# First attention of a gated two-layer block: scores and both mixes adjacent, one turn less depth, normalising on GpSimd, small inputs as rows

## The reference

```python
x = x + tanh(g_xattn[0]) * L0_xattn(ctx, layernorm(x), mask, ...)   # this step
x = x + tanh(g_ffn[0])   * L0_ffn(layernorm(x), ...)                # 16 experts
x = x + tanh(g_xattn[1]) * L1_xattn(layernorm(x), ctx, ctx, ...)
x = x + tanh(g_ffn[1])   * L1_ffn(layernorm(x), ...)

# L0_xattn: 8 heads of 64
c, l = layer_norm(ctx) * w + b, layer_norm(x') * w + b
q = l @ Wq;  k, v = split(concat([c, l]) @ Wkv)          # 128 keys per sequence
q, k = l2norm(q) * q_scale, l2norm(k) * k_scale           # per head
sim = 8 * q @ k.T, masked;  out = softmax(sim) @ v
y = layer_norm(out @ Wo) * w
```

## Time and profile before

| | |
|---|---|
| median of 3 runs | 402.84 us (402.82 to 404.82) |
| profiled execution, its time | 402.89 us |
| its span, first to last instruction | 401.1 us |
| mean granted clock of TensorE | 0.977 |
| PE, PEld busy | 370.6 (92%), 270.5 (67%) |
| DVE busy | 324.2 (81%) |
| ACT busy | 258.2 (64%) |
| POOL busy | 222.0 (55%) |
| DMA packets | 61035, 13.27 MB |

### The profile page before, as it was taken

The page is one execution under the profiler, slowest core; times in us unless marked ns, Lnnn a source line. Parts: engine busy times, 40 slices in busy tenths (PEclk is TensorE's granted clock), DMA queues, the critical chain, the costliest instruction groups (busy, mean ns, idle before and its releaser), DMA issues. The chain is left out here.

```text
span 401.1 us, 10527 instructions
## 1 busy us (share of the span) xinstructions
PE 370.6 (92%) x3589; PEld 270.5 (67%) x3589; DVE 324.2 (81%) x921; ACT 258.2 (64%) x514; POOL 222.0 (55%) x389
## 2 busy tenths in 40 slices
PE   7699989999999999999999999999799999997765
PEld 6356656666666676777756888778577777775554
DVE  2999999899889999987483788565658988887896
ACT  2477767787777777776654222344377777787784
POOL 3655668656676666663422000046738888886860
PEclk9999999999999999999999999999989999998599
DMA  5979999900000000000000000000000000000003
GB/s 162 260 145 123 124 129 126 95 2 2 0 2 2 2 2 2 1 2 2 3 2 0 2 0 0 2 2 0 2 2 2 2 2 2 3 2 2 1 15 92
DMA packets 61035, 13.27 MB, mean 33 GB/s; under 512 B 51108, under 2 KB 60344, under 8 KB 60984
## 3 DMA queue, kind: packets, MB, share of 16 engines
q1 hardware_dynamic: 60196, 12.37, 21.7%
q10 hardware_dynamic: 660, 0.23, 0.2%
q0 software_dynamic: 128, 0.00, 0.0%
HBM read 11.55 MB, written 1.05 MB: 31 GB/s over the span
## 5 line engine op out<-in xcount | busy, mean ns | idle before, releaser
L407 POOL TENSOR_TENSOR a_rn<-a_ssq,neghalf 128x8 f32<-128x8 f32 x48 | 79.0, 1654 | 23.2 <-DVE a_ssq L1019 18.6
L90 POOL TENSOR_TENSOR nrow<-mrow 128x2 f32<-128x2 f32 x32 | 6.3, 198 | 55.8 <-DVE mrow L86 55.5
L1019 DVE TENSOR_REDUCE a_ssq<-q_home 128x8 f32<-128x512 f32 x48 | 32.2, 672 | 5.4 <-ACT q_home L798 5.2
L501 PE MATMUL a_x<-wkv_a,a_kvT 128*128 128x512 f32 x64 | 34.5, 621 | 1.4 <-ACT a_kvT L791 1.0
L804 ACT ACTIVATE kv_home<-a_x,maskcol 128x512 f32<-128x512 f32 x32 | 21.9, 684 | 18.8 <-PE a_x L501 18.8
L1372 POOL TENSOR_TENSOR b_k<-b_ksb,quad 128x256 f32<-128x256 f32 x32 | 19.0, 614 | 12.0 <-ACT b_ksb L1723 12.0
L423 POOL TENSOR_TENSOR a_yr<-a_ymv,eps_row 128x1 f32<-128x1 f32 x16 | 3.1, 192 | 37.7 <-DVE a_ymv L1062 37.7
L1887 DVE TENSOR_REDUCE b_mx<-b_s 128x16 f32<-128x1024 f32 x16 | 19.6, 1224 | 5.1 <-PE b_s L1530 5.1
L1038 DVE TENSOR_REDUCE a_mx<-a_s 128x4 f32<-128x512 f32 x32 | 21.9, 685 | 2.0 <-PE a_s L527 1.9
L816 ACT ACTIVATE kv_home<-a_m,cols 128x512 f32<-128x512 f32 x32 | 21.9, 686 | 0.6 <-PE a_m L515 0.5
L546 PE MATMUL a_m<-kv_home,p_home 128*64 128x65 f32 x512 | 21.9, 228 | 0.3 <-ACT p_home L826 0.3
(11 more groups left out here) (298 smaller groups left out, 1149.6 us busy)
## 6 DMA issues: line engine op xcount, KB each, us to landing
w_gu<-in_L_ffn_Wg_dram SPq DMA_DIRECT2D x4, 512.0 KB, 9.4
w_gu<-in_L_ffn_Wu_dram SPq DMA_DIRECT2D x4, 512.0 KB, 11.5
w_d<-in_L_ffn_Wd_dram SPq DMA_DIRECT2D x8, 256.0 KB, 7.7
out_dram<-xs SPq DMA_DIRECT2D x8, 128.0 KB, 1.8
xs<-in_x_dram SPq DMA_DIRECT2D x1, 640.0 KB, 8.8
cs<-in_ctx_dram SPq DMA_DIRECT2D x1, 640.0 KB, 10.2
wkv_a<-in_L_xattn_Wkv_dram SPq DMA_DIRECT2D x2, 256.0 KB, 6.6
nat<-in_L_ffn_w_dram SPq DMA_DIRECT2D x2, 256.0 KB, 3.1
```

The costliest lines, as they stand in the source:

```text
L407: nc.gpsimd.tensor_tensor(rn[:, tp, i, :], ssq[:, tp, i, :], neghalf[:, 0:H0], ALU.pow)\
L501: nc.tensor.matmul(p_x[:], kvT[:, tp, b * 2 * S:(b + 1) * 2 * S], wkv_a[:, INNER:2 * INNER], start=True, stop=True).then_inc(vproj_done, 1)
L1019: nc.vector.tensor_reduce(ssq[:, tp, i, :], sq[:, i, :].rearrange("p (h d) -> p h d", h=H0), AX.X, ALU.add).then_inc(reduced, 1)
```

## The change

- TensorE: in a turn, both `mix` of tile s - 2 stand directly behind `scores` of tile s - 1 at the end of the turn, where the mixes of s - 3 stood apart at the start of the next. Both `probs_T` of s - 2 and `xT` of s + 1 come ahead of the scores.
- GpSimd normalises the tiles from 2 on; the mean is stored negated and added. Its powers are spread over the turn.
- VectorE's and ScalarE's lists are reordered; the squares' sums and the query scale of tile s move into turn s; `write_output`, `next_input` come one and two turns earlier, and there are 19 turns instead of 21. The statistics of the last group and the other extra work stay at the end of their turns.
- The prologue ends with operations of tiles 1 and 2 that were in the first turn.
- The mask comes once as rows and is cast into two halves of `small_rows`; the head scales are loaded as rows 32 and 33 of it, and one transpose turns them all, which now waits for the scales as well. On ScalarE's queue the masks go ahead of the second group of context.

```diff
-        maskraw = sb("maskraw", [B, 2 * S], U8)
-        mask_rows = sb("mask_rows", [B, 2 * S])
+        maskraw = sb("maskraw", [B, S], U8)
+        small_rows = sb("small_rows", [B + 2, 2 * S])
...
-        TURNS = range(2, NT + 7)
+        TURNS = range(2, NT + 5)
...
-            for i, w in ((8, q_scale), (9, k_scale)):
+            for i, w in enumerate((q_scale, k_scale)):
                 for a in range(2):
-                    pool.dma_start(cols[a * DH0:(a + 1) * DH0, i:i + 1],
-                                   w.rearrange("(d o) -> d o", o=1)).then_inc(scale_in, 16)
+                    pool.dma_start(small_rows[B + i:B + i + 1, a * DH0:(a + 1) * DH0],
+                                   w.rearrange("(o d) -> o d", o=1)).then_inc(scale_in, 16)
...
+            def normalise(t, tp):
+                wait(pool, xT_done, t - 1 if t > 2 else t)
+                nc.gpsimd.tensor_scalar(xn[:, tp, 0, :], cs[:, t, :], moments[:, 0, t, 0:1], moments[:, 0, t, 1:2],
+                                        ALU.add, ALU.mult)
+                nc.gpsimd.tensor_scalar(xn[:, tp, 1, :], xs[:, t, :], moments[:, 1, t, 0:1], moments[:, 1, t, 1:2],
+                                        ALU.add, ALU.mult).then_inc(xn_ready, 1)
+
             inverse_roots(0)
             inverse_roots(1)
             for i in range(3):
                 inverse_norm(0, 0, i)
-            inverse_roots(2)
+            pool.wait_ge(norms_ready, 2)
+            normalise(2, 0)
+            inverse_norm(1, 1, 0)
+            inverse_norm(1, 1, 1)
             for s in TURNS:
+                if exists(s - 1, NT):
+                    inverse_norm(s - 1, (s - 1) % 2, 2)
+                for i in (2, 3):
+                    if s + 1 == GROUPS[i][0]:
+                        inverse_roots(i)
+                        pool.wait_ge(norms_ready, i + 1)
+                if exists(s + 1, NT):
+                    normalise(s + 1, (s + 1) % 2)
+                if exists(s - 2, NT):
+                    weigh(s - 2, s % 2)
                 if exists(s - 4, NT):
                     add_bias(s - 4, s % 2)
-                if exists(s - 1, NT):
-                    for i in range(3):
-                        inverse_norm(s - 1, (s - 1) % 2, i)
-                if exists(s - 2, NT):
-                    weigh(s - 2, s % 2)
-                if s == 5:
-                    inverse_roots(3)
-                if exists(s - 6, NT):
-                    inverse_root(pool, s - 6).then_inc(root_ready, 1)
                 if exists(s - 4, NT):
                     out_norm(s - 4, s % 2)
+                if exists(s, NT):
+                    inverse_norm(s, s % 2, 0)
+                if exists(s - 5, NT):
+                    inverse_root(pool, s - 5).then_inc(root_ready, 1)
+                if exists(s, NT):
+                    inverse_norm(s, s % 2, 1)
...
             pe.wait_ge(masked_ready, 1)
-            nc.tensor.transpose(p_s0[:, 0:B], mask_rows[:], ident[0:B, 0:B]).then_inc(small_turned, 1)
+            pe.wait_ge(scale_in, 16 * 4)
+            nc.tensor.transpose(p_s0[:, 0:B + 2], small_rows[:], ident[0:B + 2, 0:B + 2]).then_inc(small_turned, 1)
...
+            xT(2, 0)
             scores(0, 0)
             for s in TURNS:
-                if exists(s - 3, NT):
-                    probs_T(s - 3, 1)
-                if exists(s, NT):
-                    xT(s, s % 2)
-                if exists(s - 3, NT):
-                    mix(s - 3, (s - 3) % 2, 0)
                 if exists(s - 1, NT):
                     turn_queries(s - 1, (s - 1) % 2)
-                if exists(s - 3, NT):
-                    mix(s - 3, (s - 3) % 2, 1)
-                if exists(s - 1, NT):
                     project_v(s - 1, (s - 1) % 2, 0)
                 if exists(s - 4, NT):
                     out_proj(s - 4)
...
                     probs_T(s - 2, 0)
                 if exists(s, NT):
                     project(s, s % 2, 2)
+                if exists(s - 2, NT):
+                    probs_T(s - 2, 1)
+                if exists(s + 1, NT):
+                    xT(s + 1, (s + 1) % 2)
                 if exists(s - 1, NT):
                     scores(s - 1, (s - 1) % 2)
+                if exists(s - 2, NT):
+                    mix(s - 2, s % 2, 0)
+                    mix(s - 2, s % 2, 1)
...
-            act.dma_start(cs[:, second, :], c_tiles[:, second, :]).then_inc(second_in, 16)
             act.dma_start(maskrep[:, 0:FIRST_MASKS, :], mask[0:FIRST_MASKS, :].rearrange("(o b) s -> o b s", o=1)
                           .to_broadcast([P, FIRST_MASKS, S])).then_inc(mask_in, 16)
-            for b in range(2):
-                act.dma_start(maskraw[:, b * S:(b + 1) * S], mask).then_inc(mask_in, 16)
+            act.dma_start(maskraw[:], mask).then_inc(mask_in, 16)
+            act.dma_start(cs[:, second, :], c_tiles[:, second, :]).then_inc(second_in, 16)
...
+            affine(2, 0)
             for s in TURNS:
-                if exists(s, NT):
-                    affine(s, s % 2)
-                if s == 2:
-                    open_gates()
                 if exists(s - 1, NT):
                     queries_out(s - 1, (s - 1) % 2)
                     values(s - 1, (s - 1) % 2, 0)
                 if exists(s - 2, NT):
                     exp(s - 2, 0)
+                if s == 2:
+                    open_gates()
                 if exists(s, NT):
                     square(s, s % 2, 0)
                 if exists(s - 1, NT):
                     keys_out(s - 1, (s - 1) % 2, 0)
+                    values(s - 1, (s - 1) % 2, 1)
                 if exists(s - 3, NT):
                     att_out(s - 3)
+                if exists(s - 2, NT):
+                    exp(s - 2, 1)
+                if exists(s, NT):
+                    square(s, s % 2, 1)
                 if exists(s - 1, NT):
                     keys_out(s - 1, (s - 1) % 2, 1)
-                if exists(s, NT):
-                    square(s, s % 2, 1)
-                if exists(s - 2, NT):
-                    exp(s - 2, 1)
-                if exists(s - 1, NT):
-                    values(s - 1, (s - 1) % 2, 1)
                 if exists(s - 2, NT):
                     probs_out(s - 2, 0)
                 if exists(s, NT):
                     square(s, s % 2, 2)
                 if exists(s - 2, NT):
                     probs_out(s - 2, 1)
+                if exists(s + 1, NT):
+                    affine(s + 1, (s + 1) % 2)
...
-                nc.vector.tensor_scalar(moments[:, :, r, 0], m_sum, 0.5, None, ALU.mult)
+                nc.vector.tensor_scalar(moments[:, :, r, 0], m_sum, -0.5, None, ALU.mult)
...
-                dve.wait_ge(mask_in, 16 * 3)
-                nc.vector.tensor_copy(mask_rows[:], maskraw[:]).then_inc(masked_ready, 1)
+                dve.wait_ge(mask_in, 16 * 2)
+                for a in range(2):
+                    last = nc.vector.tensor_copy(small_rows[0:B, a * S:(a + 1) * S], maskraw[:])
+                last.then_inc(masked_ready, 1)
...
+                nc.vector.tensor_copy(cols[:, 8:10], p_s0[:, B:B + 2])
                 for b in range(2):
                     last = nc.vector.tensor_copy(maskcol[b * S:(b + 1) * S, b:B:2], p_s0[b * S:(b + 1) * S, b:B:2])
                 last.then_inc(maskcol_ready, 1)
-                dve.wait_ge(scale_in, 16 * 4)
...
+            reduce(1, 1, 0)
             find_other_masked()
-            later = sum(GROUPS[3]) // 2
+            reduce(1, 1, 1)
+            scale(1, 1, 0)
+            reduce(1, 1, 2)
             for s in TURNS:
-                if exists(s - 1, NT):
-                    reduce(s - 1, (s - 1) % 2, 0)
-                if exists(s, NT):
-                    for i, (first, _) in enumerate(GROUPS):
-                        if s == first:
-                            dve.wait_ge(norms_ready, i + 1)
-                    normalise(s, s % 2)
-                if exists(s - 1, NT):
-                    reduce(s - 1, (s - 1) % 2, 1)
-                if exists(s - 5, NT):
-                    write_output(s - 5, (s - 5) % 2)
-                if exists(s - 1, NT):
-                    scale(s - 1, (s - 1) % 2, 0)
                 if exists(s - 2, NT):
                     row_max(s - 2, 0)
                 if exists(s - 1, NT):
-                    reduce(s - 1, (s - 1) % 2, 2)
                     scale(s - 1, (s - 1) % 2, 1)
                 if exists(s - 2, NT):
-                    shift(s - 2, 0)
+                    row_max(s - 2, 1)
                 if exists(s - 3, NT):
                     attend(s - 3, 0)
                     attend(s - 3, 1)
+                if exists(s - 2, NT):
+                    shift(s - 2, 0)
+                if exists(s - 4, NT):
+                    read_output(s - 4, s % 2)
+                if exists(s - 1, NT):
+                    scale(s - 1, (s - 1) % 2, 2)
                 if exists(s, NT):
                     replace_masked(s, s % 2)
-                if exists(s - 2, NT):
```

(26 more changed lines are left out.)

6 lines of the change are left out of this document (4 added, 2 removed).

## The result

The changed kernel takes 408.15 us (median of 4 runs, 405.81 to 410.96) against 402.83 for the kernel before beside it: a ratio of 1.0105, interval 1.0057 to 1.0154. Two more groups of twelve runs gave 1.0083 (1.0041 to 1.0125) and 1.0091 (1.0050 to 1.0131). It is slower by about 1%, outside the forecast's range. The profiled execution took 407.97 us for a span of 406.1.

What follows compares the result with a forecast made beforehand. TensorE's issue plus its losses between kinds of work was taken as the bound. Start -1.8, first turns +0.8, turns 9 to 15 -1.3 and end +2.0 gave -0.3, so 402.6 us; range 397.5 to 406.0.

Steps and rivals of the forecast that it cites:

- The turn order: TensorE's full turn in the first attention: summed spacings give 10.51 us against 10.79, or 10.61 with the bank wait.
- x: TensorE's loss going from 64x64 scores straight to 128x64 mixes: taken as 0.12 us, between 0.04 and 0.19.
- bank wait: Second probabilities' transposes on TensorE wait for ScalarE's key copy, now behind square(s, 1): 0.1 us a turn, 0 to 0.2.
- stretch "that keeps its order": TensorE from the first value projection to the second key projection within a turn: taken over unchanged at 6.30 us.
- The start, -1.8: Prologue: mask lands earlier, so VectorE's cast starts near 7.8 instead of 9.74; gain 1.8 us, ends 0 and 2.5.
- the rival in which the start gains nothing: Prologue: context or scale rows land at 9.9, so no gain there, the rest as summed: 404.4 us, chance 0.08.
- The first turns, +0.8: Early turns: VectorE's extra work delays shift, exp, key copy and scores directly; cost 0.8 us, 0 to 2.5.
- The end, +2.0: Value projection of tile 15 to last out_proj: 17.5 us instead of 15.5, nothing left to fill waits; +1 to +3.
- Behind the first attention, nothing: After the last out_proj TensorE runs the same gapless list to the logits, so no time was added.
- round through VectorE: Rival in full turns: this chain, put at 10.1 us with 0.5 to spare, becomes the bound; 406.5 us, chance 0.34 0.13.
- GpSimd blocked nobody: Rival in full turns: GpSimd's normalising passes hold VectorE for 0.93 us, making the round 11.0; 408 us, chance 0.05.
- The faster rival: Turns of 10.5 us, nothing lost in the first turns, end costs only 1.2: 398.4 us, chance 0.34.

Runs made afterwards that it cites:

- the experiment with the gap: Changed kernel with VectorE's extra work of turns 2 to 7 moved ahead of scale(s, 0), where VectorE waits for GpSimd's power: 405.08 us, ratio 1.0037.
- the first tail order: Changed kernel with VectorE's order changed in turns 16 and 17, and TensorE turning the first probabilities ahead of the attended values: 408.46 us, ratio 1.0125.
- the delayed kernel before: Kernel before the change with 26 extra identity transposes on TensorE ahead of the scores of tile 0: 409.27 us, ratio 1.0117.
- the key copy: Changed kernel with ScalarE's copy of the turned keys ahead of square(s, 1) again: 406.53 us, ratio 1.0065.
- both: Changed kernel with VectorE's extra work moved into its wait for GpSimd's power and ScalarE's key copy ahead of the second squares: 403.51 us, ratio 0.9991.
- the filler: Changed kernel with twenty idle-filling identity transposes ahead of TensorE's three waits in the last turn but one of scores: 408.27 us, ratio 1.0116.
- the two fastest: Changed kernel with extra work moved into VectorE's wait, key copy first and context ahead of masks: 402.89 us; the same with a reordered tail: 401.42 us.

## Why the prediction was wrong

The forecast was no change, 402.6 us, and the kernel is slower, by 3.9 to 5.3 us in the medians of three groups of runs. Three steps failed. The gain at the start and the cost of the first turns were each mis-sized by 1.6, and the work behind the first attention was put at nothing ("TensorE runs the same gapless list to the logits"), where the clock took 2.8 to 3.3 in the three profiles of this kernel. Term by term, with the points of the table above:

**The turn order, 10.51 with x at 0.12, plus 0.1 of bank wait.** The turn is 10.51, 0.1 better than forecast, by two errors. x is 0.18 (1.03 less 0.85), nearly the 0.19 of leaving the scores altogether, and mix to mix costs next to nothing. Both agree with what the Trainium skill (TensorEngine Tiling (Array Packing), Key Properties) says, that a change of mode drains the engine and a change of tile alone doesn't. The sum with x at 0.19 was 10.58. The bank wait is 0.18 and not 0.1. Against these, the stretch "that keeps its order" is 6.08 (123.79 to 129.87), not 6.30: in its old place the value projection came behind a mix and the first key projection behind a short wait, 0.10 and 0.11 that I carried along. So turns 9 to 15 brought -2.13, not -1.3.

**The start, -1.8.** Measured -0.24 in this profile, and about -0.35 by the means of two profiles of the old start (15.40 and 14.95) and the eight of the new one. This step failed. The cast did come earlier, at 7.14, but VectorE then stood 2.20 for the context that had been issued behind the masks, and TensorE 0.48 for the scale rows. I had the context at 8.2 "when VectorE wants it"; it came at 9.8. This was the rival in which the start gains nothing, at 0.08 of chance, and the bound of 9.9 for the late landing stood in the text. With the context first and the masked keys ahead of its wait, the start came about 0.7 earlier.

**The first turns, +0.8.** Measured +2.38, near the upper bound of 2.5. The mechanism was the one written down, and the experiment with the gap returned 2.2 of it. The walk mis-sized it: it let the slack of 0.5 absorb the extra work turn by turn, while the trace shows that the wait for the queries' power (1.16 in turn 4) comes first and the statistics behind it. Scores of tile 4 came at 68.15 instead of 66.2.

**The end, +2.0.** Measured 18.21 us instead of the forecast 17.5, so +2.71; 6.67 to the scores of tile 15 for 6.1, because of a wait of 0.96 for the exponential of tile 14's second half, and 11.54 for 11.4. Where the 18.21 go is read from the waits; no experiment got them back cleanly.

**The sum.** Schedule: -0.24 + 2.38 - 2.13 + 2.71 = +2.72 at the last output projection, where I had -0.3. Of the 3.0 between, 1.6 is the start and 1.6 the first turns, 0.7 the end, and 0.8 came back in the full turns. The two further profiles of this kernel stand at 194.16 and 193.80, so +2.2 to +2.7. Even with +2.72 the time would have been 405.6, inside the range.

**Behind the first attention, nothing.** This is the step that took the time out of the range. The medians lie 3.9 to 5.3 over the kernel before, by the ratios 3.3 to 4.2, against 2.2 to 2.7 of schedule. All three profiles of this kernel have the low stretch at 201 (13.63 to 14.12 us from the last output projection to the mean of the weights, for 10.84), and lack the one at 290 (1.5) that the kernel before has.

Every run of the two larger groups comes with its mean granted clock, and this tells more than the medians. In both kernels the time rises as it falls, by about 0.25 us for each 0.001: beside the second group the kernel before takes 401.4 us at 0.983 and 406.5 at 0.966 (medians). A straight line through the 88 runs of these groups puts the changed kernel 3.3 us (2.8 to 3.8) above the kernel before at the same mean clock. Its mean clock is 0.002 lower, which is the other 0.5 of the 3.8 between the means. So 0.6 to 1.1 us is left over the schedule at equal clock. That it comes from the place of the low stretches is argued, not shown: the place shifts between executions and kernels, and what decides it isn't known.

**The rivals.** The round through VectorE did not become the bound of the full turns, and GpSimd blocked nobody; the kernel came out slower through the first turns and the end. The faster rival was right about turns of 10.5, and wrong about everything around them.

## What to carry to other kernels

When a pipeline loses a stage, once-only work that used to end a turn may now stand ahead of the operation that everything waits for: look for the wait in the round and put it there. A transfer that moves up in a queue moves another down; ask who waits for that one, and give it its landing time under the new order, not the issue delay alone. A gain per turn is small change beside the fill and the drain: here 2.1 us over seven turns against 5.1 lost in the first turns and the drain, and the same instructions in another order gave 7 us of the median back (408.33 to 401.42).

## What the runs showed of the hardware

- TensorE's clock falls to 1.2 GHz for 3 to 7 us at least once before 300 us in every profile of this program, but not at a fixed place: at 201 to 208 in the changed kernel (three times) and with normalising moved back, at 200 to 207 with the first tail order, at 204 to 211 in the delayed kernel before; near 290 in the kernel before, with the gap, with the key copy and with both, at 295 with the filler; at the start (12 to 18, 13 to 17, 16 to 20) in three, two of which are among those just named; at 196 to 202 and 183 to 187 in the two fastest. It fell behind full stretches and behind thin ones. At the start it cost 0.9 us and 1.2 (filler left out), at 201 2.8 to 3.3, at 290 1.5. It falls in every profile again between 367 and 391, for 7 to 14 us in all, and between 390 and 411; what that costs isn't worked out here. What decides the place is open.
- The landing of a transfer depends on what stands ahead of it in its queue: the 128 KB of context took 3.0 to 3.2 us from issue to landing ahead of the masks, and 6.2 to 7.0 behind them.
- A pair of fp32 matmuls in different modes side by side, 64x64 scores and 128x64 mixes, costs 0.18 us at the border; two mix groups side by side cost 0.04.
- An fp32 matmul of the identity, 128x128, runs as two of 0.11 us, while a transpose of the same size is one.
